# A fused GRU stack and FFN on one core: where the last layer's variances are computed

## Time and profile before

| What | Value |
|---|---|
| median of 3 runs | 1541.29 us (1541.26 to 1541.32) |
| the profiled execution | 1541.36 us, span of its instructions 1539.5 us |
| TensorE busy | 1519.3 us, 99% of the span |
| VectorE busy | 1337.0 us, 87% |
| ScalarE busy | 1022.7 us, 66% |
| GpSimd busy | 1010.9 us, 66% |
| granted TensorE clock | 1.000 of full speed |

### The profile page before, as it was taken

The page is one execution under the profiler, slowest core; times in us unless marked ns, Lnnn a source line. Parts: engine busy times, 40 slices in busy tenths (PEclk is TensorE's granted clock), DMA queues, the critical chain, the costliest instruction groups (busy, mean ns, idle before and its releaser), DMA issues.

```text
span 1539.5 us, 22931 instructions
## 1 busy us (share of the span) xinstructions
PE 1519.3 (99%) x7744; PEld 1203.2 (78%) x7744; DVE 1337.0 (87%) x1893; ACT 1022.7 (66%) x1688; POOL 1010.9 (66%) x1141
## 2 busy tenths in 40 slices
PE   9999999999999999999999999999999999999999
PEld 7887888888888888888888877777777777777776
DVE  8998999999899989999888888786878888787877
ACT  7988789898687897787987444445444444444354
POOL 6766657578868678676788655565665666565566
PEclk9999999999999999999999999999999999999999
DMA  4211212321312112122044541030202020111001
GB/s 171 76 38 67 105 54 90 123 70 63 124 41 83 58 39 90 68 90 89 29 146 143 195 167 42 1 110 0 91 20 89 21 89 22 62 48 41 29 15 41
DMA packets 73157, 113.20 MB, mean 74 GB/s; under 512 B 5193, under 2 KB 37961, under 8 KB 69970
## 3 DMA queue, kind: packets, MB, share of 16 engines
q1 hardware_dynamic: 72754, 111.21, 21.2%
q10 hardware_dynamic: 288, 0.52, 0.1%
HBM read 73.95 MB, written 37.77 MB: 73 GB/s over the span
## 4 chain that ended last, share of the span: by engine, by line
PE 51%; DVE 2%; ACT 1%; issue 0%; POOL 0%; DVEq 0%; ACTq 0%; POOLq 0%
PE ps L639 15%; PE ps L620 15%; PE ps L572 11%; PE ps L499 6%; PE ps L519 1%; PE ps L585 1%; PE ps L533 1%; PE ps L649 1%; PE ps L662 0%; DVE bnp L1132 0%; ACT H L876 0%; DVE yb L1112 0%; DVE H L1120 0%; ACT AH L880 0%; DVE H L1121 0%
## 5 line engine op out<-in xcount | busy, mean ns | idle before, releaser
L499 PE MATMUL ps<-AH,WH 128*128 128x512 f32 x896 | 367.0, 410 | 7.8 <-DVE H L1121 6.1
L499 PE MATMUL ps<-AL,WH 128*128 128x512 f32 x896 | 351.1, 392 | 0.0
L499 PE MATMUL ps<-AH,WL 128*128 128x512 f32 x896 | 349.4, 390 | 0.0
L1687 POOL TENSOR_TENSOR acq<-acq,sq 128x512 f32<-128x512 f32 x120 | 182.4, 1520 | 153.7 <-ACT sq L963 153.1
L1572 POOL TENSOR_TENSOR H<-H,yb 128x512 f32<-128x512 f32 x192 | 246.2, 1293 | 8.4 <-DVE yb L1112 1.3
L1112 DVE TENSOR_TENSOR_SCAN yb<-ab,ps 128x512 f32<-128x512 f32 x192 | 232.1, 1209 | 15.8 <-POOL ab L1563 9.4
L950 ACT ACTIVATE g<-ps 128x512 f32<-128x512 f32 x128 | 76.6, 598 | 250.4 <-PE ps L620 250.4
L837 ACT ACTIVATE yb<-ps,ncnd 128x512 f32<-128x512 f32 x224 | 158.5, 707 | 86.7 <-PE ps L499 83.9
L1307 DVE SCALAR_TENSOR_TENSOR gl<-g,wbcol,gh 128x512 fp32r<-128x512 f32 x118 | 125.3, 1062 | 94.3 <-ACT gh L960 93.5
L499 PEld LDWEIGHTS ps<-AH,WH 128*128 128x128 f32 x896 | 168.5, 188 | 46.7 <-DVE H L1121 8.7
L499 PEld LDWEIGHTS ps<-AL,WH 128*128 128x128 f32 x896 | 168.1, 188 | 37.1
(11 more groups left out here) (193 smaller groups left out, 3212.4 us busy)
## 6 DMA issues: line engine op xcount, KB each, us to landing
hs_scratch<-H SPq DMA_DIRECT2D x16, 1024.0 KB, 5.4
hc<-hs_scratch SPq DMA_DIRECT2D x32, 512.0 KB, 4.2
xr<-in_x SPq DMA_DIRECT2D x32, 256.0 KB, 4.4
out<-ob SPq DMA_DIRECT2D x32, 256.0 KB, 2.2
xbuf<-in_x SPq DMA_DIRECT2D x7, 1024.0 KB, 7.5
RAW<-in_wt SPq DMA_DIRECT2D x16, 256.0 KB, 6.3
stg<-in_fct SPq DMA_DIRECT2D x16, 256.0 KB, 3.1
stg<-in_pjt SPq DMA_DIRECT2D x16, 256.0 KB, 2.8
```

What stands on the lines that cost most here:

```text
L499: r = e.matmul(GATE[i % 3][:], w[:, q, m * 128:(m + 1) * 128], a[:, q, :], start=(n == 0), stop=(n == 11))
L1687: e.tensor_tensor(acq[b % 2][:], acq[b % 2][:], sq[:], ALU.add).then_inc(f_s2, 1)
```

## The change

For batches 1 to 7, `tokens`, `stats` and `inv` of layer 3 are left out of the stack (`turned(t)` is false for them). In their place each of the 28 units 4 to 31 gets, in the FFN:

- ScalarE: `state_squares(u)`, the square of hc, 128 x 1024, into hsq.
- GpSimd: `state_sums(u, 0)` from hc and `state_sums(u, 1)` from hsq. Each is two additions: the four feature blocks of both directions in pairs (512 elements a partition out), then the two pairs (256 out). Four such results stand in hsum.
- TensorE: `spread(u)`, four 128 x 128 transposes of hsum into the bank TURNED, directly behind `fc`.
- VectorE: `factors(u)`, a sum over the 128 features in each of the four blocks (from PSUM, 128 x 512 to 128 x 4) and three instructions on 128 x 2, behind `low_part`.
- GpSimd: `state_factors(u)`, the power -1/2 into `rl` (128 x 2), ahead of `squares`.

```diff
+def squared_at(b, c):
+    u = 4 * b + {1: 5, 4: 6, 7: 7, 13: 8}.get(c, 4 * NB)
+def added_at(b, c):
+    u = 4 * b + {2: 5, 5: 6, 8: 7, 14: 8}.get(c, 4 * NB)
+def spread_at(b, c):
+    u = 4 * b + {(0 if b > 0 else 1): 4, 4: 5, 7: 6, 10: 7}.get(c, 4 * NB)
+def turned(t):
+    return t[2] < 3 or t[0] == 0
...
 def tokens(tau, pr):        # and the same in stats and inv
-            if tau is None:
+            if tau is None or not turned(TAILS[tau]):
                 return
...
+        def spread(u):
+            b, n = (u - 4) // 4, u - 4
+            e.wait_ge(f_hs, 4 * n + 4)
...
+            for k in range(4):
+                r = e.transpose(TURNED[:, k * 128:(k + 1) * 128], hsum[:, k, :], ident[:])
+            r.then_inc(f_ht, 1)
...
-        tokens(LAST, 0)
-        tokens(LAST, 1)
...
             fc(j)
+            if spread_at(b, c) is not None:
+                spread(spread_at(b, c))
...
+            e.activation(hsq[:], hc[i][:], ACT.Square).then_inc(f_hq, 1)
...
             hidden(j)
+            if squared_at(b, c) is not None:
+                state_squares(squared_at(b, c))
...
+        def factors(u):
+            n, r = u - 4, u % 2
+            e.wait_ge(f_ht, n + 1)
+            e.reduce_sum(htot[:, r, :], TURNED[:].rearrange("p (k n) -> p k n", k=4), axis=AX_X).then_inc(f_hr, 1)
+            e.wait_ge(f_hr, n + 1)
+            e.scalar_tensor_tensor(hmean[:, r, :], htot[:, r, 0:2], 1.0 / 512 ** 2, htot[:, r, 0:2], ALU.mult,
+                                   ALU.mult).then_inc(f_hm, 1)
+            e.tensor_scalar(hve[:, r, :], htot[:, r, 2:4], 1.0 / 512, EPS, ALU.mult, ALU.add).then_inc(f_he, 1)
...
+            e.tensor_tensor(hvar[:, r, :], hve[:, r, :], hmean[:, r, :], ALU.subtract).then_inc(f_hv, 1)
...
-        stats(LAST, 0)
         unit_lo(3)
-        stats(LAST, 1)
...
             low_part(j)
+            if spread_at(b, c) is not None:
+                factors(spread_at(b, c))
...
+            e.wait_ge(f_hs, k)
+            e.tensor_tensor(pair, src[:, :, 0:2, :], src[:, :, 2:4, :], ALU.add).then_inc(f_hs, 1)
+            e.wait_ge(f_hs, k + 1)
...
+            e.tensor_tensor(hsum[:, 2 * of_squares:2 * of_squares + 2, :], pair[:, :, 0, :], pair[:, :, 1, :],
+                            ALU.add).then_inc(f_hs, 1)
...
+            e.tensor_tensor(rl[:, u // 4, :, u % 4], hvar[:, r, :], nhalf[:, 0:2], ALU.pow).then_inc(f_rl, 1)
...
-        inv(LAST, 0)
-        inv(LAST, 1)
         addx(4)
+        state_sums(4, 0)
+        state_sums(4, 1)
         for j in range(NB * NC):
...
+            if spread_at(b, c) is not None:
+                state_factors(spread_at(b, c))
+            if added_at(b, c) is not None:
+                state_sums(added_at(b, c), 0)
+            if c > 0 and added_at(b, c - 1) is not None:
+                state_sums(added_at(b, c - 1), 1)
             squares(j)
```

More of the change, by code:

```diff
@@ L45 @@
 FUSE_AT = (2, 5, 8, 11)
+def squared_at(b, c):
+    u = 4 * b + {1: 5, 4: 6, 7: 7, 13: 8}.get(c, 4 * NB)
+    return u if u < NU else None
+def added_at(b, c):
+    u = 4 * b + {2: 5, 5: 6, 8: 7, 14: 8}.get(c, 4 * NB)
+    return u if u < NU else None
+def spread_at(b, c):
+    u = 4 * b + {(0 if b > 0 else 1): 4, 4: 5, 7: 6, 10: 7}.get(c, 4 * NB)
+    return u if u < NU else None
 JOBS = [
@@ L172 @@
         _i = subject(_who, _s - _o)
-        if _i is not None and _what == "T":
-            USERS += [("T", _i, _n, 0), ("T", _i, _n, 1)]
+        if _what == "T":
+            USERS += [] if _i is None or not turned(TAILS[_i]) else [("T", _i, _n, 0), ("T", _i, _n, 1)]
         elif _i is not None and (_who == "x" or TAILS[_i][2] < 3):
@@ L308, in pixart_block @@
     sg = sb(p2, "sg", [128, 2, 4])
-    sb(p2, "pad", [128, 336])
+    htot = sb(p2, "htot", [128, 2, 4])
+    hmean = sb(p2, "hmean", [128, 2, 2])
+    hvar = sb(p2, "hvar", [128, 2, 2])
+    hve = sb(p2, "hve", [128, 2, 2])
+    sb(p2, "pad", [128, 304])
     x18 = sb(p2, "x18", [128, 512])
@@ L325, in pixart_block @@
     xh.append(sb(p2, "xh1", [128, KC, S], F32R))
-    glx = sb(p2, "glx", [128, 4, S], F32R)
+    with ExitStack() as p4:
+        glx = sb(p4, "glx", [128, 4, S], F32R)
+    with ExitStack() as p5:
+        hsq = sb(p5, "hsq", [128, 8, 128])
+        hpair = sb(p5, "hpair", [128, 4, 128])
+        hsum = sb(p5, "hsum", [128, 4, 128])
+    sb(p2, "under", [128, 4, S])
     gh = [sb(p2, f"gh{i}", [128, S], F32R) for i in range(3)]
@@ L390, in pixart_block @@
     f_rd = sem("f_rd")
+    f_hq, f_hs, f_ht, f_hr, f_hm, f_he, f_hv, f_rl = (
+        sem(n) for n in ("f_hq", "f_hs", "f_ht", "f_hr", "f_hm", "f_he", "f_hv", "f_rl"))
     f_ma, f_mp = sem("f_ma"), sem("f_mp")
@@ L583, in feat @@
                 e.wait_ge(f_rd, 2 * (u // 4) - 3)
+            if u >= 4:
+                e.wait_ge(f_hr, u // 4 * 4 - 4 + min(u % 4 + 2, 4))
             for m in range(KC):
@@ L586, in feat @@
             r.then_inc(f_t1, 1)
+        def spread(u):
+            b, n = (u - 4) // 4, u - 4
+            e.wait_ge(f_hs, 4 * n + 4)
+            if n % 4 == 0:
+                e.wait_ge(f_xh, u)
+                e.wait_ge(f_xl, u)
+            elif n % 4 == 1 and b > 0:
+                e.wait_ge(f_rd, 2 * b - 1)
+            elif n % 4 == 1:
+                e.wait_ge(f_hr, n)
+            else:
+                e.wait_ge(f_xh, u - 1)
+                e.wait_ge(f_xl, u - 1)
+            for k in range(4):
+                r = e.transpose(TURNED[:, k * 128:(k + 1) * 128], hsum[:, k, :], ident[:])
+            r.then_inc(f_ht, 1)
         def fc_of_first(t):
@@ L929, in whole, with state_squares @@
             e.activation(hch[i][:], hc[i][:], ACT.Copy).then_inc(f_sh, 1)
+        def state_squares(u):
+            i, n = u % 2, u - 4
+            e.wait_ge(d_hc[i], 16 * (u // 2) + 16)
+            if n == 0:
+                e.wait_ge(d_hs[3], 64)
+            else:
+                e.wait_ge(f_hs, 4 * n - 1)
+            e.activation(hsq[:], hc[i][:], ACT.Square).then_inc(f_hq, 1)
         def unit_feat(u):
@@ L1117, in scan @@
                 e.wait_ge(d_hs[s + 1], stored((b - 2, 1, 3)))
-                e.wait_ge(s_t1, max(T1N[("T", TAIL[(b - 2, i, 3)], p, 1)] for i in (0, 1) for p in (0, 1)) + 1)
+                if b == 2:
+                    e.wait_ge(s_t1, max(T1N[("T", TAIL[(0, i, 3)], p, 1)] for i in (0, 1) for p in (0, 1)) + 1)
             e.tensor_tensor_scan(H[s][:, m, :], ab[c][:], GATE[c][:], 0.0, ALU.mult, ALU.add).then_inc(s_sf, 1)
@@ L1668, in addx, with state_sums, state_factors @@
             e.tensor_tensor(xr[i][:], xr[i][:], fbb[:], ALU.add).then_inc(f_xf, 1)
+        def state_sums(u, of_squares):
+            n, k = u - 4, 4 * (u - 4) + 2 * of_squares
+            src = (hsq if of_squares else hc[u % 2])[:].rearrange("p (d q) t -> p d q t", d=2)
+            pair = hpair[:].rearrange("p (d q) t -> p d q t", d=2)
+            if of_squares:
+                e.wait_ge(f_hq, n + 1)
+            else:
+                e.wait_ge(d_hc[u % 2], 16 * (u // 2) + 16)
+                if n == 0:
+                    e.wait_ge(d_hs[3], 64)
+            e.wait_ge(f_hs, k)
+            e.tensor_tensor(pair, src[:, :, 0:2, :], src[:, :, 2:4, :], ALU.add).then_inc(f_hs, 1)
+            e.wait_ge(f_hs, k + 1)
+            if n > 0 and not of_squares:
+                e.wait_ge(f_ht, n)
+            e.tensor_tensor(hsum[:, 2 * of_squares:2 * of_squares + 2, :], pair[:, :, 0, :], pair[:, :, 1, :],
+                            ALU.add).then_inc(f_hs, 1)
+        def state_factors(u):
+            n, r = u - 4, u % 2
+            e.wait_ge(f_hv, n + 1)
+            e.tensor_tensor(rl[:, u // 4, :, u % 4], hvar[:, r, :], nhalf[:, 0:2], ALU.pow).then_inc(f_rl, 1)
         def inv_1(u):
```

22 lines of the change are left out of this document (17 added, 5 removed).

## The result

| Kernel | Median (range, runs) | Ratio to before, 95% interval |
|---|---|---|
| before | 1541.3 us (1541.26 to 1541.38, 4) | |
| changed | 1589.9 us (1588.2 to 1590.5, 4) | 1.031 (1.030 to 1.033) |

The direction was as forecast. The time lies 33 us above the forecast of 1556.7 and outside its range of 1538 to 1570. The loss over before is 48.6 us where 15.4 were forecast. The timelines are those of one execution of each kernel, 1541.4 and 1588.2 us here. Two executions of later kernels that took 3406 and 7271 us are left out of all that follows.

What follows compares the result with a forecast made beforehand. The prediction took TensorE's own instruction count as the bound. Its terms, -18.5 - 1.0 + 12.2 + 16.8 + 5.9 = +15.4 us on 1541.36, gave 1556.8, as a median 1556.7 us; range for 8 in 10: 1538 to 1570.

Steps and rivals of the forecast that it cites:

- Stack: Layer-3 `tokens` calls removed from the stack: 22.9 us of TensorE, 4.4 given back as waits, 18.5 gained (bounds 14 to 22.9).
- The 0.6 in each of six slots: Slots behind layer-3 jobs: 1.76 us removed against 1.17 of slack, so 0.6 us returns as a new wait.
- Between the stages: Last two calls' 16 transposes bring nothing; TensorE's wait for `resid(4, 0)` shrinks: 1.0 us gained (bounds 0 and 1.77).
- Spread: Four transposes behind `fc` for each of 28 units, 0.44 us each, all on TensorE's path: 12.2 us added.
- Boundary: GpSimd's sums late for `spread` in chunk 0: TensorE waits 2.8 us at six batch boundaries, 16.8 us (bounds 7.2 to 27).
- the walk: Boundary additions followed one by one from 1137.85, GpSimd and VectorE alternating; block sum ends 1144.8, TensorE goes on at 1144.9.
- Chunks 4 to 9: GpSimd's late sums make `spread` of chunk 7 wait 0.7 us and `resid` 0.2: 5.9 us in all (bounds 0 and 14).
- paragraph on ScalarE's squares and the loads: FFN: 28 squares of at most 1.2 us fall into ScalarE's waits; reads of hc delay `load_unit` by less than its lead.
- TensorE's count decides: Rival: all waits on `spread` are hidden, -7.3 us, so 1534.0; chance 0.14.
- GpSimd goes first each time: Rival: the boundary costs 1.2 us each time and chunks 4 to 9 nothing, so 1541.3, the same; chance 0.08.
- the stack keeps nothing: Rival: ScalarE and the scans set the stack's slots, removed transposes turn into waits, so 1575; chance 0.08.

Runs made afterwards that it cites:

- experiment 3: Changed kernel with SP's stores two places later and the sums of each next batch's first unit in chunks 11 and 12: 1548.9 us.
- experiment 5: Reorderings of GpSimd's work on the changed kernel with stores later; the run meant, boundary's sums in chunks 13 and 14, finals not moved: 1556.0 us.
- experiment 1: Two single edits of the changed kernel: SP's stores two places later, 1563.6 us; square of unit 4b+6 from chunk 4 to 5, 1564.0 us.

## Why the prediction was wrong

**Stack: near in size, partly by luck.** Predicted 18.5, seen 17.1. TensorE's busy time up to the first fusion matmul is 22.5 us less (22.9 were forecast), and its idle time there is 5.4 more (4.4 forecast). But the idle time did not come where it was worked out. The 0.6 in each of six slots was to be a wait for the sigmoid and the scan behind it, and TensorE waits no longer for scans than before. The new waits are those of the back-transposes for ScalarE's norm (before, then changed):

```profile
PE ps L533 <- ACT ntok L849: 1.9, 7, 0.3
...
PE ps L567 <- ACT ntok L904: 6.7, 10, 1.8
```

Three of them, 1.84, 1.49 and 1.49 us long, are most of it.

**Between the stages: wrong sign, 2.5 us.** TensorE's wait for `resid(4, 0)` shrank as forecast, though to 1.16 and only in batch 0. The wait for the normalised unit grew from 0.28 to 2.22 us, as said, but the forecast had no fall of the clock behind it:

```profile
875.91 0.66 PE L621 MATMUL ps<-ident,n 128*128 128x128 f32 x4 [2.22 <-DVE n L1371]
```

From there to the first full `fc` it is 4.74 us, before it was 3.22. These 1.5 us are the whole term.

**Spread: right** (0.44 forecast, 0.45 seen).

**Boundary: right.** Turns, durations and place were those of the walk: 2.47 waited and 2.7 lost for 2.8 forecast. Without the two falls of the clock the six would cost 16.1 where 16.8 were forecast; with them it is 19.3. That it was the chain on GpSimd, and not the fusion, is shown by moving its pieces. The Trainium skill's "SBUF — State Buffer", section "Who interferes with whom", says that a VectorE instruction with two SBUF inputs contends with a GpSimd instruction that reads SBUF. The additions agree with that: 1.72 us where VectorE gets between, 1.29 where not.

**Chunks 4 to 9: the mechanism that I walked was right and its place taken by another.** The late additions of chunks 6 and 7 cost 1.26 us a batch where 0.9 was forecast, and they can be seen once the stall is gone. The step of the prediction that failed is its paragraph on ScalarE's squares and the loads: the squares "fall into its waits", and the reads of hc hold back `load_unit`, "but by less than the buffers' half a batch of lead". I costed 28 squares by their length and their place between GELUs, and asked whether they delay a load. I never asked when each square's input is there. Four squares a batch read hc, and one of them was put 10 us ahead of the first reader that the order of before has. Both rows needed were in the trace of before: the load's issue at 1084.64 and its first use at 1093.02. The stall is 5.0 us a batch, 30.1 us in all, where the forecast had nothing for it. One fall of the clock is in each of the six. Taking the wait away at either end brings 26.3 and 25.8 us in the medians, 24.8 and 23.6 between the profiled executions. Of the 30.1, 7.6 come out from behind it again; the falls at the boundaries, one fewer in the first of the two, are most of what is left.

**The rivals.** "TensorE's count decides" (1534.0) is what the kernel becomes once the orders of SP and GpSimd fit: 1539.1. Of the 5 us above, 4 are the stack and the place between the stages, whose gain is 15.5 and not 19.5, and 0.8 are in the loop. "GpSimd goes first each time" is excluded by the 1.72 us additions at the boundary, and "the stack keeps nothing" by the run with the stack alone.

**What stays open:** how much of each stall is the clock by itself. The 1.6 comes from the boundaries and the 1.2 from stalls with one fall more; no run has the stall without a fall. In batch 2, TensorE's wait of 3.43 and one fall of 1.6 would make up the 5.0, but that is a sum and not a test.

## What to carry to other kernels

When an instruction is added to an in-order queue, look up the landing time of its input at the new place, in the trace of before, for every repetition of the pattern, and follow that input back through the issuing queue: here what stood ahead of the DMA there set the time, not the free buffer. A blocking instruction on an engine with 66% load can cost more than the whole change gives: here 30.1 us against the 17.1 of the stack. Where several late pieces share an engine, curing the first shows the next (stall, then chunk 7, then chunk 14), so terms found behind a stall are to be added and not taken as refuted.

## What the runs showed of the hardware

**The same wait may or may not bring the clock down, with the same instructions.** In the stack, the wait of 1.84 us at 253 is new with the change. TensorE waits the same time in the changed kernel and in that of experiment 3, whose stacks are identical. Windows of the first, then of the second:

```profile
254.00:258.00 4.00, 4.00 (x21) 3.31 (x20) 2.40 (x4) 3.92 (x9) 3.02 (x3) 1.00 0.00 0
```
```profile
254.00:258.00 4.00, 4.00 (x12) 3.15 (x12) 2.41 (x4) 2.79 (x6) 2.79 (x3) 0.57 0.00 0
```

In the second the clock is at 0.57 and 12 matmuls start where 21 did. Its last stack matmul starts 1.5 us later (851.11 for 849.59). Four of the eleven profiles with the change's stack that can be compared show this fall, and their first GELU of the loop stands at 882.4 to 882.5. In the other seven it stands at 880.8 to 881.7. At the wait of 2.2 us between the stages nine of the eleven show a fall. The two without it (the stack alone, and the run of experiment 5 with the boundary's sums in chunks 13 and 14 and the finals not moved) have one at 8 us, and their stacks end within 0.3 us of those of the four.

At the boundaries, the same wait of some 2.5 us is followed by a fall in 9 of 24 cases: 2 of 6 in the changed kernel, 1 and 2 in the two runs of experiment 1, 4 in that with the old stack. The Trainium skill, page "TensorE: Matmul & The Clock Gate", part 1, says that what grants the clock runs free of the kernel, so that the same kernel meets it at another phase. The two profiles agree with that, and no run here shows more of it. The runs of the version with the finals later lie from 1544.0 to 1546.4, the 17 of before beside them from 1541.2 to 1541.8. That such waits make the scatter is likely but not shown.
